# Pool multiplies the scan's states with C two at a time, with a ring of eight states

## The chip, the core and the metric

The kernel runs on one NeuronCore of a Trainium2 chip. The core has five engines with queues of their own: PE (TensorE, matrix multiply), DVE (VectorE), ACT (ScalarE), Pool (GpSimd) and SP (SyncE, which here issues all transfers). They meet by semaphores. The metric is device time in microseconds (us). The kernel before takes 12802.62 us (median of 3 runs, 12800.36 to 12805.07).

## The reference

The input is x of 8 images x 96 channels x 64 x 64 in float32. Layer 0 is a group norm, then a vision state-space block: layer norm, a projection to 192 channels and a gate, a depthwise 3x3 convolution, a selective scan along four directions, an output norm, gate and projection, and a small channel-attention convolution branch. Layer 1 is a linear attention and a feed-forward whose operands are rounded to an 8-bit float. The change lies in the selective scan and in where one weight is kept. The scan:

```python
def selective_scan(xs, dts, A, Bs, Cs, Ds, dt_bias):
    delta = jax.nn.softplus(dts + dt_bias[None, :, :, None])
    ...
    def step(h, inp):
        u_t, d_t, b_t, c_t = inp
        dA = jnp.exp(d_t[..., None] * A)
        h = dA * h + (d_t * u_t)[..., None] * b_t[:, :, None, :]
        y = jnp.einsum('bkdn,bkn->bkd', h, c_t)
        return (h, y)
    _, ys = jax.lax.scan(step, h0, (u_l, d_l, B_l, C_l))
    y = jnp.moveaxis(ys, 0, -1)
    return y + Ds[None, :, :, None] * xs
```

There are K = 4 directions (along rows, along columns, and both backwards), 192 channels, 16 states per channel and 64 x 64 = 4096 positions per image.

## The kernel before, in words

The eight images follow each other. For each, `prep_a` (norms, input projection) and `prep_b` (convolution, and the projection with w_xp that gives B, C and the low-rank dts) run, then `scan`, then `post` (all the rest). Each is a block at whose end the engines meet. w_xp (128 x 640 float32, the weights of the second projection) is built once in the setup on DVE (L434) and stays in SBUF.

`scan` makes six passes T over the 4096 positions, in four chunks of 1024: 128 channels by rows (T = 0) and by columns (T = 1), then the remaining 64 channels of both directions together (T = 2), and the same three backwards (3 to 5). T = 1 and 4 are called column-wise below. In a chunk g each of the 16 states n goes through these steps; a tile is 128 channels x 1024 positions.

- ACT: exp of delta times A[n] (`decay`, L1110), for the states in POOLED = (2, 5, 7, 10, 13, 15) into a PSUM bank instead. Exp n waits for scan n - 2. Behind exp n stands the copy of the last column of state n - 1 (`carry`, L1087), which Pool waits for, so that the multiply with C cannot overwrite it. Behind exp 3 and carry 2 stand a table load, the softplus of the next chunk and a table load back (L1093); behind exp 5 the copy of the previous chunk's y (L1080).
- B[n] times du: for ten states PE spreads the row of B over the partitions (L994) and DVE multiplies it by du (L1158). For the six in POOLED the row comes from memory by a broadcasting transfer into `b_sb` and Pool multiplies it (L1191, into `dbu`, two buffers).
- DVE: `tensor_tensor_scan` over the 1024 positions (L1171), into `state`, a ring of RING = 7 tiles. It waits until PE has added up the state that was in the slot.
- Pool: state times C[n] in place (L1202), with the row of C from memory in `c_sb` (a ring of CRING = 4). SP loads the row of n once the multiply of n - 4 is done (L942, in passes 2 and 5 two transfers of 64 partitions, L946).
- PE: adds the products of the 16 states in PSUM with an identity matmul (L1017), in an order given by SUMS_AT, six steps behind the scans and later.

du of the next chunk (delta times u, L1141) is made by DVE in front of scan 8 (DU_AT), and delta is copied by ACT after exp 9 (L1101). Both have two buffers. All orders are written out in the code, by the place of each call in the loops over n. Lines of the kernel before are used below; names such as "scan 10", "exp 4" and "carry 3" mean the instruction of that state, C(2,3) Pool's multiply of states 2 and 3, B10 Pool's B product for state 10.

Of the kernel before, what the change touches and what calls it, by code (L numbers as in the profile page):

```python
# [55 lines left out]
RING = 7  # L56
CRING = 4
# [3 lines left out]
B_AHEAD = 4  # L61
# [3 lines left out]
DU_AT = 8  # L65
# [42 lines left out]
def build(nc, x, weights, phase_weights, setup_weights, out, gate_dram, gn_dram):  # L108
    bc_dram = nc.dram_tensor("bc", (NDIR, 2, NS, L), F32, kind="Internal").ap()
# [28 lines left out]
    w_xp = put("w_xp", [128, 5, 128], F32)  # L138
# [52 lines left out]

    conv_diag = at("conv_diag", [128, PE_TAPS, 128], F32, C0 + 512 + 20480)
# [26 lines left out]
    delta, du, decay, state, c_sb, b_sb, dbu = (scan_buf(n, r) for n, r in (("delta", 2), ("du", 2), ("decay", 2), ("state", RING), ("c_sb", CRING),  # L219
# [44 lines left out]
    with ExitStack() as ctx:  # L264
# [9 lines left out]
        dbu_pooled scanned carried weighted summed y_summed y_taken c_in_0 c_in_1 c_in_2 c_in_3 b_in_0  # L274
# [91 lines left out]
        with nc.Block() as block:  # L366
            @block.sync
            def _(sp):
# [6 lines left out]
                sp.wait_ge(S["w_loaded"], 80 + 16 * GROUPS)  # L375

# [9 lines left out]
            def _(dve):  # L386
# [40 lines left out]
                for g in range(2):  # L427
                    for order in range(2):
                        places = ((w3, order, order, 0, 128), (w3, 2 + order, 2, DR * order, DR * order + DR))
                        for from_, i, src, lo_p, hi_p in places + (((w3_up, 4, 2, DR, 128),) if order == 0 else ()):  # L430
                            for to, st, first, count in ((NS * g, 2 * g, 3 * NS * order, NS),
                                                         (C_ROW + NS * g, 2 * g + 1, 3 * NS * order, NS),
                                                         (DT0 + RANK * g, 2 * g + order, 6 * NS, RANK)):
                                nc.vector.tensor_copy(w_xp[lo_p:hi_p, i, to:to + count],  # L434
                                                      from_[lo_p:hi_p, st, src, first:first + count])
# [76 lines left out]
        def prep_a(img):  # L512
            bank = dict(zip(("turn0", "turn1", "mean", "za", "var", "halo", "xi", "mix"), sum(ps, [])))
            with nc.Block() as block:  # L514
                @block.sync
                def _(sp):
# [4 lines left out]

                    sp.wait_ge(S["gn_ready"], NCH)
# [70 lines left out]
                def _(pe):  # L593
# [300 lines left out]
        def scan():  # L894
# [27 lines left out]
            def slot(g, n):  # L922

                return (g * NS + n) % RING

            def c_landed(T, c, n):

                before = sum(32 if t % 3 == 2 else 16 for t in range(T)) * (NSC * NS // CRING)
                return (c * (NS // CRING) + (n // CRING + 1)) * (32 if T % 3 == 2 else 16) + before

# [5 lines left out]
            with nc.Block() as block:  # L936
                @block.sync
                def _(sp):
# [11 lines left out]
                    def steps(T, c, previous, following):  # L950
# [4 lines left out]
                        for n in range(NS):  # L955
# [3 lines left out]
                            sp.wait_ge(S["weighted"], g * NS + n - CRING + 1 + CREDIT)  # L959
                            spread_row(T, at, 1, n, c_sb[:, n % CRING, :], f"c_in_{n % CRING}")  # L960
# [25 lines left out]
                def _(pe):  # L986
# [24 lines left out]
                    def add_up(g, n):  # L1011
# [3 lines left out]
                        pe.wait_ge(S["weighted"], g * NS + n + 1 + CREDIT)  # L1015
# [48 lines left out]
                def _(act):  # L1064
# [731 lines left out]
```

## Time and profile before

| What | us or share |
|---|---|
| profiled execution, its own time | 12802.17 |
| its span in the trace | 12800.4 |
| PE busy | 10530.1 (82%) |
| DVE busy | 11326.4 (88%) |
| ACT busy | 6529.3 (51%) |
| Pool busy | 10358.3 (81%) |
| Pool, state times C (L1202), 3072 recorded | 7180.6, mean 2375 ns |
| Pool, B times du (L1191), 1152 | 2731.8, mean 2371 ns |
| DVE, B times du (L1158), 1920 | 2320.3, mean 1208 ns |
| DVE, the scans with a carry and a decay tile (L1171), 1440 | 3378.3, mean 2346 ns |
| TensorE's granted clock, mean | 0.896 |

The busy shares are means over an image's stages, the scan and the rest. The mean of an instruction is from its start to its end as the profiler draws it; consecutive instructions of one engine can overlap there, so what one costs in a row is read from the distance of starts. PE's rows show two speeds of the same matmul, since its clock is granted at either of two levels.

### The profile page before, as it was taken

The numbers are of one execution on the slowest core, as the hardware profiler recorded it, in microseconds if no ns is written. First come the engines' busy times: TensorE is split into PE (matmuls) and PEld (weight loads), VectorE is DVE, ScalarE is ACT, GpSimd is POOL, SyncE is SP. The second block draws the span as 40 slices with busy tenths as digits, with TensorE's granted clock in tenths as the row PEclk, the third lists the DMA queues.
The fourth block names the chain that finished last, engine by engine and source line by source line (L and its number), as shares of the span: only waits on it lengthen the run. The fifth ranks groups of instructions, "written<-read, shape, count | busy, mean of one in ns | idle before, by whom it ended". The sixth has DMA issues, their size and how long they took to land. (4 is left out here: it accounts for less than half of the span.)

```text
span 12800.4 us, 92077 instructions
## 1 busy us (share of the span) xinstructions
PE 10530.1 (82%) x24646; PEld 4148.3 (32%) x24646; DVE 11326.4 (88%) x8071; ACT 6529.3 (51%) x9780; POOL 10358.3 (81%) x4597
## 2 busy tenths in 40 slices
PE   7888888788887888878888788887888888888888
PEld 2333333333333332333323333233332333333333
DVE  7999779997899978999789997899978999689996
ACT  4445455454544555455555455554555445554455
POOL 5999559994599946999469994699946999469993
PEclk9888989989899898988988889899998888989888
DMA  5787547775478744777447774577745777357773
GB/s 147 225 227 227 124 136 226 228 226 120 144 224 229 225 114 150 223 229 226 109 151 227 228 226 107 157 226 228 225 102 163 226 229 225 95 165 224 227 227 95
DMA packets 734712, 2403.47 MB, mean 188 GB/s; under 512 B 173200, under 2 KB 175248, under 8 KB 722768
## 3 DMA queue, kind: packets, MB, share of 16 engines
q1 hardware_dynamic: 734192, 2397.58, 64.5%
q8 instruction: 199, 3.26, 0.1%
q14 instruction: 321, 2.63, 0.1%
HBM read 2300.18 MB, written 67.11 MB: 185 GB/s over the span
## 5 line engine op out<-in xcount | busy, mean ns | idle before, releaser
L1202 POOL TENSOR_TENSOR state<-state,c_sb 128x1024 f32<-128x1024 f32 x3072 | 7180.6, 2375 | 71.5 <-ACT carry L1087 52.0
L1017 PE MATMUL ps<-state,wt 128*128 128x512 f32 x12288 | 6354.9, 660 | 160.9 <-ACT ya L1080 97.4
L1017 PEld LDWEIGHTS ps<-state,wt 128*128 128x128 f32 x12288 | 2564.7, 212 | 3074.0 <-issue 2483.9
L1171 DVE TENSOR_TENSOR_SCAN state<-decay,carry,ps 128x1024 f32<-128x1024 f32 x1440 | 3378.3, 2346 | 117.2 <-DVE ps L1158 72.9
L1087 ACT COPY carry<-state 128x1 f32<-128x1 f32 x3072 | 584.3, 190 | 4925.5 <-DVE state L1171 4919.1
L1191 POOL TENSOR_TENSOR dbu<-b_sb,du 128x1024 f32<-128x1024 f32 x1152 | 2731.8, 2371 | 174.3 <-DVE du L1176 174.3
L994 PE MATMUL ps<-parts,sel 114*128 114x512 bf16 (+1 forms) x3840 | 1325.0, 431 | 1658.6 <-DVE state L1171 1642.0
L1158 DVE TENSOR_TENSOR ps<-ps,du 128x1024 f32<-128x1024 f32 x1920 | 2320.3, 1208 | 26.2 <-PE ps L994 23.2
L1110 ACT ACTIVATE decay<-delta,a_neg 128x1024 f32<-128x1024 f32 x1920 | 2198.4, 1145 | 3.4 <-issue 0.3
L1171 DVE TENSOR_TENSOR_SCAN state<-ps,carry,dbu 128x1024 f32<-128x1024 f32 x864 | 2013.9, 2331 | 69.4 <-POOL dbu L1191 56.0
L994 PEld LDWEIGHTS ps<-parts,sel 114*128 114x128 bf16 (+1 forms) x3840 | 281.4, 102 | 3169.8 <-DVE state L1171 2713.5
L1110 ACT ACTIVATE ps<-delta,a_neg 128x1024 f32<-128x1024 f32 x1152 | 1283.5, 1114 | 0.0
L1171 DVE TENSOR_TENSOR_SCAN state<-decay,ps 128x1024 f32<-128x1024 f32 x480 | 1097.2, 2286 | 50.4 <-DVE ps L1158 24.3
L1518 POOL CAST h<-h16b 128x1536 fp8e5<-128x1536 f16 x64 | 116.0, 1812 | 895.9 <-DVE h16b L1643 895.9
L1171 DVE TENSOR_TENSOR_SCAN state<-ps,dbu 128x1024 f32<-128x1024 f32 x288 | 654.5, 2273 | 43.8 <-POOL dbu L1191 38.5
L302 ACT ACT_TABLE_LOAD x409 | 524.7, 1283 | 71.2 <-DMA x_tok<-x 26.9
L1504 POOL TENSOR_TENSOR sqa<-sqa,sqr 64x512 f32<-64x512 f32 x64 | 101.9, 1593 | 412.0 <-ACT sqr L1412 412.0
L1006 PE MATMUL ps<-parts,dt_w 114*128 114x512 bf16 (+1 forms) x1536 | 377.2, 389 | 43.4 <-PEq L659 29.9
L502 ACT ACTIVATE rs<-ps,wt 96x512 f32<-96x512 f32 (+1 forms) x320 | 218.4, 683 | 318.7 <-PE ps L487 172.3
L492 DVE TENSOR_TENSOR cen<-x,ps 96x512 f32<-96x512 f32 x192 | 130.6, 680 | 249.4 <-PE ps L487 248.7
L487 PE MATMUL ps<-sq,wt 96*96 96x512 f32 x512 | 281.7, 633 | 23.3 <-ACT sq L497 22.2
L704 POOL TENSOR_SCALAR conv_acc<-pad_r,wt 128x512 f32<-128x512 f32 x8 | 12.5, 1566 | 355.2 <-POOLq L514 355.2
(209 smaller groups left out, 8812.8 us busy)
## 6 DMA issues: line engine op xcount, KB each, us to landing
c_sb<-bc SPq DMA_DIRECT2D x2048, 512.0 KB, 4.4
c_sb<-bc SPq DMA_DIRECT2D x2048, 256.0 KB, 5.7
b_sb<-bc SPq DMA_DIRECT2D x768, 512.0 KB, 4.7
b_sb<-bc SPq DMA_DIRECT2D x768, 256.0 KB, 5.6
x_nat<-x SPq DMA_DIRECT2D x17, 1536.0 KB, 14.7
gates<-gate_a SPq DMA_DIRECT2D x8, 2048.0 KB, 6.8
x_tok<-x SPq DMA_DIRECT2D x288, 48.0 KB, 1.9
gn<-gn_t SPq DMA_DIRECT2D x8, 1536.0 KB, 7.1
```

What stands on the lines that cost most here:

```text
L302: act.add_instruction(mybir.InstLoadActFuncSet(name=nc.get_next_instruction_name(), act_func_set_id=which, ins=[], outs=[]))
L487: pe.matmul(bank[0:C, :], col("ones_c", C), src[0:C, sl(j)], start=True, stop=True).then_inc(done, 1)
L502: act.activation(root[:, sl(j)], bank[0:p, :], ACT.Ln, bias=col("eps", p)).then_inc(logged, 1)
L994: mm = pe.matmul(bank[:, q * CH:(q + 1) * CH], sel[own, n, first:first + 128], part_cols(at, 2 * (T // 3), q, own), start=True, stop=True)
L1006: mm = pe.matmul(pc[:, q * CH:(q + 1) * CH], dt_w[own, p, w, :], part_cols(at, k, q, own), start=(i == 0 and p == 0), stop=(i == len(ways) ...
L1017: mm = pe.matmul(py[:, q * CH:(q + 1) * CH], col("ident"), state[:, slot(g, n), q * CH:(q + 1) * CH], start=(n == 0), stop=False)
L1087: act.copy(carry[:, n:n + 1], state[:, slot(g, n), last:last + 1]).then_inc(S["carried"], 1)
L1110: act.activation(pb[n % 2][:, :] if n in POOLED else decay[:, n % 2, :], delta[:, g % 2, :], ACT.Exp, scale=a_neg[:, T, n:n + 1]).then_inc ...
L1158: dve.tensor_tensor(pb[n % 2][:, :], pb[n % 2][:, :], du[:, g % 2, :], ALU.mult)\
L1171: dve.tensor_tensor_scan(state[:, slot(g, n), way], rate, what, 0.0 if fresh else carry[:, n:n + 1], ALU.mult, ALU.add)\
L1191: pool.tensor_tensor(dbu[:, i % BRING, :], b_sb[:, i % BRING, :], du[:, g % 2, :], ALU.mult)\
L1202: pool.tensor_tensor(state[:, slot(g, n), :], state[:, slot(g, n), :], c_sb[:, n % CRING, :], ALU.mult).then_inc(S["weighted"], 1)
```

## The change

Pool takes two states in one instruction of 128 x 2048, once the carries of both have been copied. The ring of states has eight tiles, so a pair is always adjacent; C rows come in a ring of three pairs, and the semaphores `weighted` and `c_in_*` count pairs. Room for this comes from delta and du, of which there is one buffer each: du of the next chunk is made in front of scan 15, when Pool's B15 is done, and delta is copied after exp 15. The first B product of a chunk (state 2) moves to the end of the previous one, ahead of C(14,15). B rows are asked for five steps ahead rather than four. The larger scan buffers lie over w_xp, so it is stored to memory once in the setup and loaded again by SP in each `prep_a`, and the first input projection waits for that load with the others. With one buffer, L1158 and L1110 read `du[:, :]` and `delta[:, :]`; such lines are left out here.

```diff
-RING = 7
-CRING = 4
+RING = 8
+PAIR = 2
+CRING = 6
-B_AHEAD = 4
+B_AHEAD = 5
-DU_AT = 8
...
+                sp.wait_ge(S["setup_dve"], 7)
+                sp.dma_start(xp_dram, w_xp[:, :, :].rearrange("p i c -> p (i c)")).then_inc(S["w_loaded"], 16)
+                sp.wait_ge(S["w_loaded"], 96 + 16 * GROUPS)
...
+                    sp.dma_start(w_xp[:, :, :].rearrange("p i c -> p (i c)"), xp_dram).then_inc(S["w_in_loaded"], 16)
...
-                            pe.wait_ge(S["w_in_loaded"], 64)
+                            pe.wait_ge(S["w_in_loaded"], 80)
...
-                            sp.wait_ge(S["weighted"], g * NS + n - CRING + 1 + CREDIT)
-                            spread_row(T, at, 1, n, c_sb[:, n % CRING, :], f"c_in_{n % CRING}")
+                            sp.wait_ge(S["weighted"], pair_of(g, n) - CRING // PAIR + 1 + CREDIT)
+                            spread_row(T, at, 1, n, c_sb[:, PAIR * c_place(g, n) + n % PAIR, :], f"c_in_{c_place(g, n)}")
...
-                        pe.wait_ge(S["weighted"], g * NS + n + 1 + CREDIT)
+                        pe.wait_ge(S["weighted"], pair_of(g, n) + 1 + CREDIT)
...
-                        act.wait_ge(S["decayed"], max(g - 1, 0) * NS)
-                        act.copy(delta[:, g % 2, :], pc[:, :]).then_inc(S["delta_ready"], 1)
+                        act.wait_ge(S["decayed"], g * NS)
+                        act.copy(delta[:, :], pc[:, :]).then_inc(S["delta_ready"], 1)
...
-                                if n == DU_AT + 1:
+                                if n == NS - 1:
                                     delta_out(g + 1)
...
-                        dve.wait_ge(S["dbu_pooled"], (g - 1) * NP + CREDIT)
+                        dve.wait_ge(S["dbu_pooled"], g * NP + CREDIT)
...
-                            if n == DU_AT and after:
+                            if n == NS - 1 and after:
                                 next_du(*after, g + 1)
...
-                            if n + 2 in POOLED:
+                            if n > 0 and n + 2 in POOLED:
                                 times_b(T, c, POOLED.index(n + 2))
-                            pool.wait_ge(S["carried"], g * NS + n + 1 + CREDIT)
-                            pool.wait_ge(S[f"c_in_{n % CRING}"], c_landed(T, c, n))
-                            pool.tensor_tensor(state[:, slot(g, n), :], state[:, slot(g, n), :], c_sb[:, n % CRING, :],
-                                               ALU.mult).then_inc(S["weighted"], 1)
-
+                            if n == NS - 1 and following:
+                                times_b(*following, 0)
+                            if n % PAIR == PAIR - 1:
+                                times_c(T, c, n - PAIR + 1)
+
+                    def times_c(T, c, n):
+
+                        g = c + T * NSC
+                        pool.wait_ge(S["carried"], g * NS + n + PAIR + CREDIT)
+                        pool.wait_ge(S[f"c_in_{c_place(g, n)}"], c_landed(g, n))
+                        first = PAIR * c_place(g, n)
+                        both = state[:, slot(g, n):slot(g, n) + PAIR, :]
+                        pool.tensor_tensor(both, both, c_sb[:, first:first + PAIR, :], ALU.mult)\
+                            .then_inc(S["weighted"], 1)
```

Pool's order over one chunk of the kernel before, from the B product of state 2 (`dbu`) on:

```order
L1191 TENSOR_TENSOR dbu<-b_sb,du 128x1024
L1202 TENSOR_TENSOR state<-state,c_sb 128x1024 x3
L1191 TENSOR_TENSOR dbu<-b_sb,du 128x1024
L1202 TENSOR_TENSOR state<-state,c_sb 128x1024 x2
L1191 TENSOR_TENSOR dbu<-b_sb,du 128x1024
L1202 TENSOR_TENSOR state<-state,c_sb 128x1024 x3
L1191 TENSOR_TENSOR dbu<-b_sb,du 128x1024
L1202 TENSOR_TENSOR state<-state,c_sb 128x1024 x3
L1191 TENSOR_TENSOR dbu<-b_sb,du 128x1024
L1202 TENSOR_TENSOR state<-state,c_sb 128x1024 x2
L1191 TENSOR_TENSOR dbu<-b_sb,du 128x1024
L1202 TENSOR_TENSOR state<-state,c_sb 128x1024 x3
```

And of the changed kernel, from B5, behind C(0,1), to the pair after the next chunk's B2 (its x2 are C(14,15) and the next C(0,1)):

```order
L1207 TENSOR_TENSOR dbu<-b_sb,du 128x1024
L1228 TENSOR_TENSOR state<-state,c_sb 128x2048
L1207 TENSOR_TENSOR dbu<-b_sb,du 128x1024
L1228 TENSOR_TENSOR state<-state,c_sb 128x2048 x2
L1207 TENSOR_TENSOR dbu<-b_sb,du 128x1024
L1228 TENSOR_TENSOR state<-state,c_sb 128x2048
L1207 TENSOR_TENSOR dbu<-b_sb,du 128x1024
L1228 TENSOR_TENSOR state<-state,c_sb 128x2048
L1207 TENSOR_TENSOR dbu<-b_sb,du 128x1024
L1228 TENSOR_TENSOR state<-state,c_sb 128x2048
L1207 TENSOR_TENSOR dbu<-b_sb,du 128x1024
L1228 TENSOR_TENSOR state<-state,c_sb 128x2048 x2
```

Sixteen multiplies have become eight, B2 has moved in front of C(14,15), and nothing stands between C(14,15) and C(0,1), nor between C(4,5) and C(6,7).

DVE around the du of the next chunk, before: from scan 6 over scan 7, multiply 8, du (`ps2` holds softplus's output) and scan 8 to multiply 9 and its scan.

```order
L1171 SCALAR_TENSOR_TENSOR state_103<-decay_102,carry_63,ps0 128x1024
L1171 SCALAR_TENSOR_TENSOR state_103<-ps1,carry_63,dbu_106 128x1024
L1158 TENSOR_TENSOR ps0<-ps0,du_101 128x1024
L1141 TENSOR_TENSOR du_101<-ps2,ua_81 128x1024
L1171 SCALAR_TENSOR_TENSOR state_103<-decay_102,carry_63,ps0 128x1024
L1158 TENSOR_TENSOR ps1<-ps1,du_101 128x1024
L1171 SCALAR_TENSOR_TENSOR state_103<-decay_102,carry_63,ps1 128x1024
```

The changed kernel, from scan 12 to scan 0 of the next chunk, which begins a pass and so takes no carry:

```order
L1187 SCALAR_TENSOR_TENSOR state_103<-decay_102,carry_63,ps0 128x1024
L1187 SCALAR_TENSOR_TENSOR state_103<-ps1,carry_63,dbu_106 128x1024
L1174 TENSOR_TENSOR ps0<-ps0,du_101 128x1024
L1187 SCALAR_TENSOR_TENSOR state_103<-decay_102,carry_63,ps0 128x1024
L1157 TENSOR_TENSOR du_101<-ps2,ua_81 128x1024
L1187 SCALAR_TENSOR_TENSOR state_103<-ps1,carry_63,dbu_106 128x1024
L1174 TENSOR_TENSOR ps0<-ps0,du_101 128x1024
L1187 SCALAR_TENSOR_TENSOR state_103<-decay_102,ps0 128x1024
```

The du now stands between scan 14 and scan 15. ACT around softplus, in the changed kernel, from exp 3 to carry 3:

```order
L1126 ACTIVATE decay_102<-delta_100,a_neg_54 128x1024
L1103 COPY carry_63<-state_103 128x1
L304 ACT_TABLE_LOAD
L1109 ACTIVATE ps2<-ps2,wt_49 128x1024
L304 ACT_TABLE_LOAD
L1126 ACTIVATE decay_102<-delta_100,a_neg_54 128x1024
L1103 COPY carry_63<-state_103 128x1
```

This piece is as before but for its line numbers: carry 3 (the last row) stands behind exp 4.

## Rows read from the trace of the kernel before

**Rows 1.** Windows, image 1's scan: us, each engine's busy us, PEclk, DMA share, GB/s

```profile
186.00:1410.00 1224.00, 1000.67 (x2270) 390.05 (x2270) 1183.44 (x646) 609.38 (x887) 1210.63 (x524) 0.88 0.77 227
```

**Rows 2.** The timeline (start, us, instruction, idle before): first du, last copy

```profile
187.22 1.22 DVE L1176 TENSOR_TENSOR du<-ps,ua 128x1024 f32<-128x1024 f32 x1 [3.47 <-ACT ps L1093]
...
1425.50 1.01 ACT L1077 COPY y<-ps 64x1024 f32<-64x1024 f32 x1
...
11338.48 1.23 DVE L1176 TENSOR_TENSOR du<-ps,ua 128x1024 f32<-128x1024 f32 x1 [3.42 <-ACT ps L1093]
...
12576.83 1.01 ACT L1077 COPY y<-ps 64x1024 f32<-64x1024 f32 x1
```

**Rows 3.** The timeline of Pool, one chunk of pass 2

```profile
698.23 2.33 POOL L1191 TENSOR_TENSOR dbu<-b_sb,du 128x1024 f32<-128x1024 f32 x1
...
723.63 2.33 POOL L1191 TENSOR_TENSOR dbu<-b_sb,du 128x1024 f32<-128x1024 f32 x1
...
749.03 2.33 POOL L1191 TENSOR_TENSOR dbu<-b_sb,du 128x1024 f32<-128x1024 f32 x1
```

**Rows 4.** The timeline of DVE, the same chunk

```profile
700.60 2.34 DVE L1171 TENSOR_TENSOR_SCAN state<-ps,carry,dbu 128x1024 f32<-128x1024 f32 x1
...
709.87 2.33 DVE L1171 TENSOR_TENSOR_SCAN state<-ps,carry,dbu 128x1024 f32<-128x1024 f32 x1
...
717.37 2.35 DVE L1171 TENSOR_TENSOR_SCAN state<-decay,carry,ps 128x1024 f32<-128x1024 f32 x1 [0.55 <-DVE ps L1158]
...
725.99 2.35 DVE L1171 TENSOR_TENSOR_SCAN state<-ps,carry,dbu 128x1024 f32<-128x1024 f32 x1 [0.53 <-POOL dbu L1191]
...
729.50 1.22 DVE L1141 TENSOR_TENSOR du<-ps,ur 128x1024 f32<-128x1024 f32 x1
730.64 2.34 DVE L1171 TENSOR_TENSOR_SCAN state<-decay,carry,ps 128x1024 f32<-128x1024 f32 x1
...
736.40 2.33 DVE L1171 TENSOR_TENSOR_SCAN state<-ps,carry,dbu 128x1024 f32<-128x1024 f32 x1
...
751.40 2.34 DVE L1171 TENSOR_TENSOR_SCAN state<-ps,carry,dbu 128x1024 f32<-128x1024 f32 x1
```

**Rows 5.** The timeline of ACT, DVE, Pool around scan 4 of a chunk

```profile
358.48 1.15 ACT L1110 ACTIVATE decay<-delta,a_neg 128x1024 f32<-128x1024 f32 x1
359.54 0.17 ACT L1087 COPY carry<-state 128x1 f32<-128x1 f32 x1
...
359.72 2.35 DVE L1171 TENSOR_TENSOR_SCAN state<-decay,carry,ps 128x1024 f32<-128x1024 f32 x1 [0.55 <-DVE ps L1158]
...
359.79 2.34 POOL L1202 TENSOR_TENSOR state<-state,c_sb 128x1024 f32<-128x1024 f32 x1 [0.22 <-ACT carry L1087]
```

**Rows 6.** The timeline of DVE, a column-wise du

```profile
526.12 1.95 DVE L1141 TENSOR_TENSOR du<-ps,ua 128x1024 f32<-128x1024 f32 x1
```

**Rows 7.** The timeline of Pool: 128, 512 and 1024 wide

```profile
52.99 2.27 POOL L530 TENSOR_TENSOR conv_diag<-wt,conv_w 128x128 f32<-128x128 f32 x5
...
105.87 1.27 POOL L715 TENSOR_TENSOR conv_acc<-conv_acc,conv_tap 128x512 f32<-128x512 f32 x1
...
188.53 2.35 POOL L1191 TENSOR_TENSOR dbu<-b_sb,du 128x1024 f32<-128x1024 f32 x1 [21.69 <-DVE du L1176]
```

**Rows 8.** The timeline of DVE, scan 2 of the first chunk

```profile
196.45 2.27 DVE L1171 TENSOR_TENSOR_SCAN state<-ps,dbu 128x1024 f32<-128x1024 f32 x1
```

**Rows 9.** The timeline of DVE, a multiply that waited for PE

```profile
339.43 1.23 DVE L1158 TENSOR_TENSOR ps<-ps,du 128x1024 f32<-128x1024 f32 x1 [1.50 <-PE ps L994]
```

**Rows 10.** The timeline of PE, the last state's sum of image 1

```profile
1420.74 1.98 PE L1017 MATMUL ps<-state,wt 128*128 128x512 f32 x4 [0.32 <-POOL state L1202]
```

**Rows 11.** The page's DMA issues: KB each, median us to landing

```profile
c_sb<-bc SPq DMA_DIRECT2D x2048, 256.0 KB, 5.7
```

**Rows 12.** The timeline of SP and PE, image 2's w_in loads and first projection

```profile
1646.38 1.81 SPq L519 DMA_DIRECT2D w_in_sb<-phase_weights  x4
...
1659.85 1.06 PE L611 MATMUL ps<-cen,w_in_sb 96*128 96x512 f32 x2
```

More of the change, by code:

```diff
@@ L190, in build @@
     gn_work = at("gn_work", [C, 352], F32, C0 + 512 + 23552)
+    w_xp = at("w_xp", [128, 5, 128], F32, C0 + 512 + 25088)
     conv_diag = at("conv_diag", [128, PE_TAPS, 128], F32, C0 + 512 + 20480)
@@ L217, in scan_buf @@
         return at(name, [128, SC] if ring is None else [128, ring, SC], F32, first)
-    delta, du, decay, state, c_sb, b_sb, dbu = (scan_buf(n, r) for n, r in (("delta", 2), ("du", 2), ("decay", 2), ("state", RING), ("c_sb", CRING),
+    delta, du = map(scan_buf, ("delta", "du"))
+    decay, state, c_sb, b_sb, dbu = (scan_buf(n, r) for n, r in (("decay", 2), ("state", RING), ("c_sb", CRING),
                                                                  ("b_sb", BRING), ("dbu", BRING)))
@@ L433, in _ @@
                                                          (DT0 + RANK * g, 2 * g + order, 6 * NS, RANK)):
-                                nc.vector.tensor_copy(w_xp[lo_p:hi_p, i, to:to + count],
-                                                      from_[lo_p:hi_p, st, src, first:first + count])
+                                last = nc.vector.tensor_copy(w_xp[lo_p:hi_p, i, to:to + count],
+                                                             from_[lo_p:hi_p, st, src, first:first + count])
+                last.then_inc(S["setup_dve"], 1)
             @block.tensor
@@ L924, in slot, with pair_of, c_place, c_landed @@
                 return (g * NS + n) % RING
-            def c_landed(T, c, n):
-                before = sum(32 if t % 3 == 2 else 16 for t in range(T)) * (NSC * NS // CRING)
-                return (c * (NS // CRING) + (n // CRING + 1)) * (32 if T % 3 == 2 else 16) + before
+            def pair_of(g, n):
+                return (g * NS + n) // PAIR
+            def c_place(g, n):
+                return pair_of(g, n) % (CRING // PAIR)
+            def c_landed(g, n):
+                each = NSC * NS // PAIR
+                return sum((32 if p // each % 3 < 2 else 64) for p in range(pair_of(g, n) + 1)
+                           if p % (CRING // PAIR) == c_place(g, n))
             def b_landed(T, c, i):
@@ L1175, in _ @@
                     dve.wait_ge(S["delta_made"], 1)
[L1176 removed]
+                    dve.tensor_tensor(du[:, :], pc[:, :], u_of(0, 0), ALU.mult).then_inc(S["du_ready"], 1)
                     each_chunk(steps)
@@ L1190, in times_b @@
                         pool.wait_ge(S["scanned"], g * NS + last + 1 + CREDIT)
-                        pool.tensor_tensor(dbu[:, i % BRING, :], b_sb[:, i % BRING, :], du[:, g % 2, :], ALU.mult)\
+                        pool.tensor_tensor(dbu[:, i % BRING, :], b_sb[:, i % BRING, :], du[:, :], ALU.mult)\
                             .then_inc(S["dbu_pooled"], 1)
```

12 lines of the change are left out of this document (6 added, 6 removed).

## The prediction

> **What bounds the kernel now.** I read the busy table first (DVE 88%, Pool 81%, both with gaps outside the scan), then the windows, then the instructions in order of time. The window over one image's scan [rows 1] has Pool busy 1210.6 of 1224 us and DVE 1183.4: in the scan Pool never rests. In the row-wise chunks shown, Pool starts the B product of state 15 at 698.23 and again at 749.03 [rows 3], a cycle of 50.80 us in which it does 16 C multiplies and 6 B products, so it starts one each 2.309 us although each is drawn 2.33 to 2.35 long: consecutive ones overlap by some 0.04. DVE is close behind: its scans wait now and then for a B product (scan 7 started at 725.99 after 0.53 idle [rows 4], 2.36 after Pool began that product). So one engine limits and the other has about 1 us of room per chunk. Whatever the change gives Pool is worth something only until DVE, or a wait between the two, comes last.
>
> From the first du of an image to its last copy of y the scan takes 1238.3 us in the first image (187.22 to 1425.50) and 1238.4 in the last (11338.48 to 12576.83) [rows 2]; over the eight the mean is 1236.3.
>
> **The pair multiply, its price.** No 128x2048 instruction is in the trace. From below and above: alone, a 1024-wide one takes 2.35 and a 512-wide one 1.27 [rows 7], 2.11 ns per element, so 1024 more elements add 2.16 to the spacing of 2.309: 4.47. From the five 128-wide ones in 2.27 (0.45 each [rows 7]) the slope is (2.309 - 0.45) / 896 = 2.07 ns, which gives 4.43. I take P = 4.455 between starts, 4.49 until it is done. The ends of the range: 4.62 if a pair saves nothing, and 4.17 if all 0.45 us of the 128-wide one were fixed cost and one of them went. Pool's own work falls from 50.80 to 8 x 4.455 + 6 x 2.309 = 49.5 us a chunk. The Trainium skill, GPSIMD Engine Reference, section 3.1, states 4497 ns for a tensor_tensor of 2048 fp32 elements on this engine. No run here shows it yet; with 4.46 in place of 4.455 the sum below would grow by 3 us.
>
> **What a pair waits for.** It starts when the carry of its second state has been copied by ACT. For states 2 and 3 this is the costly case. ACT's order there is: exp of 3, carry 2, table load, softplus, table load, exp of 4, and only then carry 3. The trace has exp 4 at 358.48, carry 3 at 359.54, scan 4 on DVE at 359.72, and Pool starting on that carry at 359.79 [rows 5]. Now Pool takes states 0, 1, 2 one by one while this goes on, so nothing is lost; after the change state 2 waits too, and the pair (2,3) starts 0.07 after scan 4.
>
> **One chunk after the change,** from scan 2 to scan 2 of the next, in DVE's spacings [rows 4]. Scan 2 to scan 4: 709.87 to 717.37, 7.50, with DVE's stall for exp 4 in it (unchanged). Then Pool's order is C(2,3), B7, C(4,5), C(6,7), B10: scan 10 can start at 0.07 + P + 2.31 + 2P + 2.37 = 18.11 after scan 4. DVE alone would need 736.40 - 717.37 = 19.03, less 1.14 for du (which leaves this place: 729.50 to 730.64) and 0.53 of idle: 17.36. So scan 10 waits about 0.75 us for its B product: the stall of the chunk. Scan 10 to scan 15 takes 15.00 (736.40 to 751.40), scan 15 to scan 2 takes 9.27 (700.60 to 709.87), and du, now ahead of scan 15, 1.14. Sum 7.50 + 18.11 + 15.00 + 9.27 + 1.14 = 51.02. With a column-wise du, 1.95 long, 1.87 between starts [rows 6], it is 51.75; the waits for PE that such chunks have now lie between scans 4 and 10 and go under the 0.75.
>
> The others on that clock (scan 2 at 0): C(0,1) 0.39 (copy of carry 1), B5 4.84, C(2,3) 7.57 after 0.42 idle, B7 12.03, C(4,5) 14.3, C(6,7) 18.8, B10 23.24, C(8,9) 25.6, B13 30.0, C(10,11) 32.3, B15 36.8, C(12,13) 39.1, next B2 43.5, C(14,15) 45.9 to 50.3, then idle 1.1 until carry 1. Every other product is in time: B13 is done 2.5 before scan 13, B15 done at 39.1 before du at 40.6.
>
> **Single delta and du.** du can be made only when B15 is done, which it is; scan 15 goes on behind it. ACT then copies delta (no longer than the 1.15 of an exp of that size [rows 5]) and makes exp 0: done some 1.22 + 2 x 1.15 + 0.2 = 3.7 after du starts, needed behind scan 15 and multiply 0, at 1.14 + (9.27 - 2.26 - 3.50) = 4.65, where 2.26 is one scan and 3.50 a multiply with its scan. Next B2 starts at 43.5, du is done at 41.9. Cost nothing beyond the moved 1.14; without the cover of scan 15 both would cost 2.3 each chunk. **Ring of eight:** scan n waits for the sum of n - 8, which PE has two steps earlier. Nothing gained but the odd wait of scan 7 for a slow first sum in column-wise chunks.
>
> **C rows three pairs deep.** Row 11 is queued on SP behind the b row of state 15, which waits for B10 to end at 25.6. In passes 2 and 5 a row is two transfers of 256 KB that land 5.7 us after issue [rows 11]: 31.3 at the soonest, and C(10,11) is due at 32.3. SP's issuing of three transfers ahead eats that; I expect it up to 1 us late, which Pool takes from the 1.5 that B15 has to du and the 1.1 idle. Elsewhere rows have over 1.5 us to spare.
>
> **w_xp.** The reload of 320 KB is fifth behind four w_in loads issued at 1646.38; the first projection that waits for all starts at 1659.85 [rows 12]. At 5.7 us for a similar transfer [rows 11] it is hidden. The store in the setup is once, SP waits for it: 5 us.
>
> **The image.** First du to scan 2: 9.23 (187.22 to 196.45 [rows 2, 8]). 23 cycles: 15 x 51.02 + 8 x 51.75 = 1179.3. In the first chunk of a pass scans start from zero and are 0.06 shorter (2.27 against 2.33 [rows 8, 4]); on the stretches where DVE leads that is 8 of them, -0.5 a time, -3.5 in all. The end: from scan 2 of the last chunk, C(14,15) ends at 48.0 (no next B2 there), PE adds both states in 2 x 1.98, less 0.1 of overlap, and add_y and y's first copy take what they take now, 1420.74 + 1.98 to 1425.50 = 2.8 [rows 2, 10]: 54.8. Total 9.23 + 1179.3 - 3.5 + 54.8 = 1239.8 against 1236.3: +3.5, times 8 = +28. To that comes PE in its slow spells: at 339.43 DVE sat 1.50 us for a spread matmul [rows 9] while Pool's backlog covered part; with DVE leading I put 1 us more an image, +8, and +5 for the setup. +41 on the profiled run's 12802.2 us (span 12800.4; the median of the runs shown is 12802.62, the same): **12843 us**.
>
> **Rivals.** *Pool's pair is cheaper, DVE alone sets the pace (faster).* If P is near 4.17, scan 10 waits for nothing: 7.50 + 17.36 + 24.27 + 1.14 = 50.27, column-wise 51.0 plus some 0.3 of PE waits. Against the forecast -0.75 x 15 - 0.45 x 8 = -15 an image, -119: 12724. Each 0.1 us of P moves the cycle by 0.3 and the kernel by 0.3 x 184 = 55 us; below P = 4.33 the result is measurably faster. For it: Pool's instructions overlap at their ends by an amount no wider row shows. Against: both slopes above.
> *A pair costs two singles (slower).* P = 4.62: cycle +0.5, +91: 12934. For it: a two-row access may restart. Against: the fixed part that the widths show.
> *The third slot comes late (slower).* In passes 2 and 5 row 11 lands over 2.5 us after it could, B15 then delays du and scan 15: about 1 us in each of 64 chunks, +64: 12907. It decides once landing plus queueing exceeds some 8 us from B10's end.
> *A wash.* The waits that I put on the path overlap with stalls Pool or PE cause now, and the gain of the ring cancels the pair's wait: 12,790 to 12,820.
>
> **Numbers.** Less than 0.2% (26 us) cannot be told from no change here. Forecast 0.45 (two thirds of it above 12828), cheaper pair 0.20, no saving 0.12, late row 0.10, a wash 0.13. That gives faster 0.20, same 0.28, slower 0.52, and a range of 12765 to 12905.
>
> **What would show it.** Pool: starts of consecutive pairs 4.455 apart; an idle of about 0.4 before C(2,3) and 1.1 before C(0,1), both released by ACT's carry. DVE: an idle of 0.75 at scan 10, released by dbu, and cycles of 51.0 and 51.7. Wrong if Pool's pairs are under 4.35 or over 4.55, if scan 10 does not wait, or if Pool waits for c_sb.

## The result, and the profile after

The changed kernel takes 12904.2 us (median of 4 runs, 12903.4 to 12906.8) against 12803.0 for the kernel before (4 runs, 12800.4 to 12805.1): ratio 1.0079, 95% interval 1.0062 to 1.0097. It is slower by 101 us. The forecast was 12843, +41, in a range of 12765 to 12905: the sign and most of the mechanism were right, but several sizes were too small, and the time lies only 0.8 us inside the end of the range.

From the page after: the busy line of the five engines, the costliest groups that the change touches (busy us, mean ns, idle before it and its main releaser), and two rows of the DMA issues (KB each, median us to landing).

```profile
PE 10357.4 (80%) x24646; PEld 4045.0 (31%) x24646; DVE 11317.5 (88%) x8071; ACT 6563.8 (51%) x9780; POOL 10155.1 (79%) x3061
...
L1228 POOL TENSOR_TENSOR state<-state,c_sb 128x2048 f32<-128x2048 f32 x1536 | 6941.6, 4525 | 354.1 <-ACT carry L1103 296.9
...
L1207 POOL TENSOR_TENSOR dbu<-b_sb,du 128x1024 f32<-128x1024 f32 x1152 | 2716.1, 2358 | 175.9 <-DVE du L1192 131.6
...
L1174 DVE TENSOR_TENSOR ps<-ps,du 128x1024 f32<-128x1024 f32 x1920 | 2320.6, 1209 | 72.8 <-PE ps L1010 70.5
...
c_sb<-bc SPq DMA_DIRECT2D x2048, 256.0 KB, 6.7
```

Pool's C multiplies fell from 7180.6 to 6941.6 us busy, but Pool now stands idle before them for 354 us (71.5 before), 297 of them for ACT's copy of a carry and 54 for rows of C (52 and 18.5 before). A 256 KB row of C lands 6.7 us after its issue, where it was 5.7 [rows 11].

The window over image 1's scan, same columns as [rows 1]:

```profile
186.00:1410.00 1224.00, 967.59 (x2253) 371.19 (x2251) 1169.94 (x643) 611.14 (x883) 1169.32 (x329) 0.92 0.76 225
```

Pool is busy 1169.3 of 1224 us and no longer 1210.6, DVE 1169.9 and no longer 1183.4. Neither engine is full: they wait for each other. Pool's timeline (start, us, instruction, idle before and releaser) in pass 2, the place of [rows 3]: C(10,11) of a chunk, then from C(0,1) of the next one on:

```profile
704.32 4.51 POOL L1228 TENSOR_TENSOR state<-state,c_sb 128x2048 f32<-128x2048 f32 x1 [0.55 <-DMA c_sb<-bc]
...
722.86 4.52 POOL L1228 TENSOR_TENSOR state<-state,c_sb 128x2048 f32<-128x2048 f32 x1 [0.45 <-ACT carry L1103]
727.35 2.35 POOL L1207 TENSOR_TENSOR dbu<-b_sb,du 128x1024 f32<-128x1024 f32 x1
729.99 4.51 POOL L1228 TENSOR_TENSOR state<-state,c_sb 128x2048 f32<-128x2048 f32 x1 [0.29 <-ACT carry L1103]
734.46 2.35 POOL L1207 TENSOR_TENSOR dbu<-b_sb,du 128x1024 f32<-128x1024 f32 x1
736.76 8.99 POOL L1228 TENSOR_TENSOR state<-state,c_sb 128x2048 f32<-128x2048 f32 x2
745.72 2.34 POOL L1207 TENSOR_TENSOR dbu<-b_sb,du 128x1024 f32<-128x1024 f32 x1
```

C(10,11) waits 0.55 us for a row, C(0,1) 0.45 and C(2,3) 0.29 us for a carry; C(4,5) and C(6,7) take 8.96 from 736.76 to B10's start, so a pair costs 4.48. DVE in the same chunk, from du to du, the place of [rows 4]:

```profile
712.04 1.20 DVE L1157 TENSOR_TENSOR du<-ps,ur 128x1024 f32<-128x1024 f32 x1
...
729.92 2.35 DVE L1187 TENSOR_TENSOR_SCAN state<-decay,carry,ps 128x1024 f32<-128x1024 f32 x1 [0.55 <-DVE ps L1174]
...
748.09 2.35 DVE L1187 TENSOR_TENSOR_SCAN state<-ps,carry,dbu 128x1024 f32<-128x1024 f32 x1 [0.83 <-POOL dbu L1207]
...
763.12 1.20 DVE L1157 TENSOR_TENSOR du<-ps,ur 128x1024 f32<-128x1024 f32 x1
```

The cycle is 51.08 us (50.80 before). C(2,3) starts 0.07 after scan 4, and scan 10 starts 18.17 after scan 4 with 0.83 of idle for B10: the chain that the prediction worked out. The same engine in the last chunk of pass 1, a column-wise one, and in the first of pass 2, where another wait shows: multiply 8 for PE's spread of its B row (the prediction knew such a wait, of multiply 14, from [rows 9]). Then PE ahead of the first of the two:

```profile
587.76 1.23 DVE L1174 TENSOR_TENSOR ps<-ps,du 128x1024 f32<-128x1024 f32 x1 [1.30 <-PE ps L1010]
...
639.03 1.23 DVE L1174 TENSOR_TENSOR ps<-ps,du 128x1024 f32<-128x1024 f32 x1 [1.43 <-PE ps L1010]
```

```profile
580.56 6.72 PE L1033 MATMUL ps<-state,wt 128*128 128x512 f32 x8 [1.43 <-ACT ya L1096]
587.12 0.60 PE L1010 MATMUL ps<-parts,sel 114*128 114x512 bf16 x2
```

Image 1 from end to end: first du, second du and last du on DVE, last copy of y on ACT, beside [rows 2].

```profile
195.05 1.22 DVE L1192 TENSOR_TENSOR du<-ps,ua 128x1024 f32<-128x1024 f32 x1 [4.35 <-ACT ps L1109]
...
248.69 1.20 DVE L1157 TENSOR_TENSOR du<-ps,ua 128x1024 f32<-128x1024 f32 x1
...
1378.39 1.20 DVE L1157 TENSOR_TENSOR du<-ps,ur 128x1024 f32<-128x1024 f32 x1
...
1444.37 1.01 ACT L1093 COPY y<-ps 64x1024 f32<-64x1024 f32 x1
```

That is 53.6 to the second du, 1129.7 for 22 cycles and 66.0 to the end. Over the eight images the means are 53.51, 1129.21 and 66.21, together 1248.9 where before had 1236.3: +12.6 an image, +101 in all. The rest of the span moved by under 4 us.

### The profile page after: what moved, and what is told of

It is laid out like the page before. It is cut to its first block and busy times, and to the rows that moved or that the text cites. A ratio compares the mean times of both kernels' runs of the same rounds, so it can differ in the third digit from the quotient of the medians.

```text
span 12905.0 us, 89007 instructions
## 1 busy us (share of the span) xinstructions
PE 10357.4 (80%) x24646; PEld 4045.0 (31%) x24646; DVE 11317.5 (88%) x8071; ACT 6563.8 (51%) x9780; POOL 10155.1 (79%) x3061
## 5 line engine op out<-in xcount | busy, mean ns | idle before, releaser
L1228 POOL TENSOR_TENSOR state<-state,c_sb 128x2048 f32<-128x2048 f32 x1536 | 6941.6, 4525 | 354.1 <-ACT carry L1103 296.9
L1033 PE MATMUL ps<-state,wt 128*128 128x512 f32 x12288 | 6212.3, 646 | 191.9 <-ACT ya L1096 94.0
L1033 PEld LDWEIGHTS ps<-state,wt 128*128 128x128 f32 x12288 | 2489.9, 207 | 3049.7 <-issue 2391.2
L1010 PE MATMUL ps<-parts,sel 114*128 114x512 bf16 (+1 forms) x3840 | 1236.0, 406 | 1905.4 <-DVE state L1187 1903.2
L1174 DVE TENSOR_TENSOR ps<-ps,du 128x1024 f32<-128x1024 f32 x1920 | 2320.6, 1209 | 72.8 <-PE ps L1010 70.5
L1187 DVE TENSOR_TENSOR_SCAN state<-ps,carry,dbu 128x1024 f32<-128x1024 f32 x864 | 2013.9, 2331 | 76.2 <-POOL dbu L1207 75.4
L1010 PEld LDWEIGHTS ps<-parts,sel 114*128 114x128 bf16 (+1 forms) x3840 | 253.6, 98 | 3402.7 <-DVE state L1187 3159.6
L1187 DVE TENSOR_TENSOR_SCAN state<-ps,dbu 128x1024 f32<-128x1024 f32 x288 | 654.2, 2272 | 68.7 <-POOL dbu L1207 67.9
L1117 ACT COPY delta<-ps 128x1024 f32<-128x1024 f32 x192 | 194.3, 1012 | 217.8 <-DVE du L1157 217.8
L493 PE MATMUL ps<-sq,wt 96*96 96x512 f32 x512 | 281.8, 633 | 23.2 <-ACT sq L503 22.1
```

The lines of the kernel that those rows point to most:

```text
L493: pe.matmul(bank[0:C, :], col("ones_c", C), src[0:C, sl(j)], start=True, stop=True).then_inc(done, 1)
L1010: mm = pe.matmul(bank[:, q * CH:(q + 1) * CH], sel[own, n, first:first + 128], part_cols(at, 2 * (T // 3), q, own), start=True, stop=True)
L1033: mm = pe.matmul(py[:, q * CH:(q + 1) * CH], col("ident"), state[:, slot(g, n), q * CH:(q + 1) * CH], start=(n == 0), stop=False)
L1174: dve.tensor_tensor(pb[n % 2][:, :], pb[n % 2][:, :], du[:, :], ALU.mult)\
L1187: dve.tensor_tensor_scan(state[:, slot(g, n), way], rate, what, 0.0 if fresh else carry[:, n:n + 1], ALU.mult, ALU.add)\
L1228: pool.tensor_tensor(both, both, c_sb[:, first:first + PAIR, :], ALU.mult)\
```

## The experiments

Twelve kernels, each timed beside the kernel before on the same chip (its medians there 12794.8 to 12796.8). Edits are on the changed kernel unless the title says otherwise. The changed kernel was not timed again beside them, and the kernel before was 6 to 8 us faster there than in the result's 12803.0; so up to 8 us of each difference to 12904.2 may come from the chip and the time and not from the edit. "In the scans" means the eight stretches from first du to last copy of y, summed in the trace. What lies outside them is the same work in all these kernels but for the store and loads of w_xp, and yet takes 2885 to 2919 us, so some 20 us of a difference between two traces can lie there. "Idle for dbu" is the idle time of DVE in front of scans and du that Pool's B products released, "idle for PE" that in front of its multiplies, both summed over the whole trace; before has 94.5 and 23.2 us, after 144.6 and 70.5.

**e1_single: the pair as two 128x1024 multiplies, each behind its own carry.**

```diff
-                        pool.wait_ge(S["carried"], g * NS + n + PAIR + CREDIT)
...
-                        pool.tensor_tensor(both, both, c_sb[:, first:first + PAIR, :], ALU.mult)\
...
+                        for i in range(PAIR):
+                            pool.wait_ge(S["carried"], g * NS + n + i + 1 + CREDIT)
...
+                            one = state[:, slot(g, n + i), :]
+                            pool.tensor_tensor(one, one, c_sb[:, PAIR * c_place(g, n) + i, :], ALU.mult)\
```

> The changed kernel with one thing undone: Pool multiplies the two states of a pair by two 128x1024 instructions, each waiting for its own carry; place in Pool's order, ring of eight, C ring, du, delta and reload stay as in the changed kernel. Theory A (the loss is the wait of a pair for its second state, on the path carry 3 - C(2,3) - B7 - C(4,5) - C(6,7) - B10 - scan 10): Pool works 22 x 2.31 = 50.8 us a chunk and is the bound again, scan 10 no longer waits 0.85, cycles fall from 51.08 to about 50.8, time near 12850 (12820 to 12870). Rival B (the moved du, the single delta and du, or the C ring cost the time, the pairs gain some): Pool's extra 1.3 us a chunk comes on top, cycles above 51.3 and time 12950 or more.

12841.96 us, ratio 1.0036 [1.0022, 1.0051]. Theory A by its time: in this order of instructions the pair costs 62 us more than two singles (58 in the scans). Pool's idle for carries went from 297 us to 4, so the wait for the second carry costs more than the 0.14 us that a pair saves. But A's "scan 10 no longer waits" did not come true: scan 10 sat 142 us for B10 with pairs and still sits 106 with singles, and Pool waits 105 us for rows of C. The place of B10 is the larger part of that stall, and the next run moves it.

**e2_b10: B10 one place earlier, in front of C(6,7).**

```diff
+                            if n == 7:
+                                times_b(T, c, POOLED.index(10))
-                            if n > 0 and n + 2 in POOLED:
+                            if n > 0 and n + 2 in POOLED and n + 2 != 10:
```

> The changed kernel with B10, Pool's B product of state 10, one place earlier: in front of C(6,7) and not behind it. Theory A (scan 10 waits because B10 stands behind four pairs): the idle at scan 10 goes, cycles by rows fall from 51.08 to 50.25 (what DVE alone needs), Pool's idle before C(0,1) nearly vanishes, column-wise chunks and pass 5 gain less since multiply 8 waits for PE there; about 15 us an image, time 12784 (12760 to 12820). Rival B (the loss sits elsewhere, in du, delta, C rows): the idle moves to another scan and the time stays within 20 us of 12904.

12749.77 us, ratio 0.9966 [0.9953, 0.9979]. DVE's two rows for scans that take a B product from Pool, with and without a carry:

```profile
L1187 DVE TENSOR_TENSOR_SCAN state<-ps,carry,dbu 128x1024 f32<-128x1024 f32 x864 | 2011.0, 2328 | 0.0
...
L1187 DVE TENSOR_TENSOR_SCAN state<-ps,dbu 128x1024 f32<-128x1024 f32 x288 | 653.1, 2268 | 2.9 <-POOL dbu L1207 2.8
```

After, the same two rows have 75.4 and 67.9 us of that idle. It is gone at the scans (14 us of it now stand before du), and the time fell by 154, to 10 us below A's range. 151 of that lie in the scans, of which 28 in the first chunks, where scan 10 had sat 4.5 us in each image, and 123 in the cycles. Scan 10's wait was worth all of its size. The changed kernel with this one call moved is faster than the kernel before.

**e3_softplus: softplus and its table loads at state 8 rather than 3.**

```diff
+SOFT_AT = 8
...
-                                if n == PRE_AT + 1:
+                                if n == SOFT_AT:
                                     softplus(following[0], g + 1)
```

> The changed kernel with ACT's table load, softplus and table load behind exp 8 and carry 7 instead of behind exp 3 and carry 2; PE's matmuls for it stay where they are. Theory A: carry 3 comes 1.4 us sooner, C(2,3) starts straight behind B5, B10 0.4 us sooner, idle at scan 10 down from 0.85 to about 0.5, the 0.55 at scan 4 moves to scan 9; cycles by rows 50.7, about 6 us an image, time 12855 (12830 to 12880). Rival (carry 3 is not on the path, Pool's order alone is): no change, 12890 to 12915.

12845.79 us, ratio 1.0037 [1.0024, 1.0050]: -58. Theory A: DVE's wait for the late exp moved to scan 9 as it said (58.2 us in all where it was 96.6 at scan 4), and scan 10's wait fell from 142 us to 116.

**e4_sp_order: B rows asked for behind both C rows of a pair, C rows ahead of the late transfers of the first chunk.**

```diff
-B_AHEAD = 5
+B_AT, NEXT_B_AT = {1: 5, 3: 7, 7: 10, 9: 13, 11: 15}, 13
...
-                            if n + B_AHEAD in POOLED:
-                                spread_b(T, at, g, POOLED.index(n + B_AHEAD))
...
+                            if n in B_AT:
+                                spread_b(T, at, g, POOLED.index(B_AT[n]))
```

> The changed kernel with another order of SP's loads: the B row of a pooled state is asked for behind both C rows of a pair and never between them (B10 from five to three steps ahead), and in the first chunk of an image the C row goes ahead of the late transfers. Nothing else moves. Theory C (of the 101 us, some 34 are the first chunk of each image, where Pool waits 3.3 us for C rows 6 and 7 queued behind a B row that waits for B5 and behind the late transfers, and some 10 are late C rows in passes 2 and 5): first chunk 53.6 down to about 50, time 12868 (12845 to 12885). Rival (the rows are late because of the transfers' own time, not their place in the queue): within 10 us of 12904.

12872.16 us, ratio 1.0060 [1.0047, 1.0073]: -32, theory C by its time. The first chunk shortened less than it said, from 53.5 to 51.4 us in the mean and not to 50: 17 us of the 32. The cycles and the end give 5 more, and the rest lies outside the scans, where the edit changes nothing. The first chunk on Pool in the changed kernel:

```profile
218.57 4.53 POOL L1228 TENSOR_TENSOR state<-state,c_sb 128x2048 f32<-128x2048 f32 x1
226.43 4.51 POOL L1228 TENSOR_TENSOR state<-state,c_sb 128x2048 f32<-128x2048 f32 x1 [3.34 <-DMA c_sb<-bc]
230.90 2.33 POOL L1207 TENSOR_TENSOR dbu<-b_sb,du 128x1024 f32<-128x1024 f32 x1
```

C(6,7) sits 3.34 us for its rows, B10 stands behind it, and DVE's scan 10 follows at 233.27 after 4.55 of idle.

**e6_reload_only: the kernel before with only the store and the reloads of w_xp.**

```diff
+                sp.dma_start(xp_dram, w_xp[:, :, :].rearrange("p i c -> p (i c)")).then_inc(S["w_loaded"], 16)
...
+                    sp.dma_start(w_xp[:, :, :].rearrange("p i c -> p (i c)"), xp_dram).then_inc(S["w_in_loaded"], 16)
```

> The kernel before, with only the store of w_xp in the setup and its reload in each image added. Theory A (the reload is hidden in every image, the store costs once): 2 to 10 us over the kernel before, and PE's first input projection of an image starts as long after the w_in loads as before (13.5 us in image 2). Rival (the reload delays each image's first projection, or the loads behind it on SP): 30 us or more over the kernel before, with PE waiting for w_xp ahead of that projection.

12797.49 against 12796.59 us, ratio 1.0002 [0.9993, 1.0011], which is -9 to +14 us: the rival's 30 is out, and A's 2 to 10 cannot be told from nothing. The reload is hidden: from an image's last copy of y to the next first du the mean is 357.2 us and was 357.1.

**e7_soft_first: e2_b10 with softplus and its table loads in front of carry 2 instead of behind it.**

```diff
+                            if following and n == PRE_AT + 1:
+                                softplus(following[0], g + 1)
                             if n > 0:
                                 carry_on(T, g, n - 1)
...
-                                if n == PRE_AT + 1:
-                                    softplus(following[0], g + 1)
```

> The changed kernel with B10 in front of C(6,7) (as in the run before this one, 12750 us) and, in addition, ACT's softplus with its two table loads one place earlier: behind exp 3 and in front of carry 2. Theory A: exp 4 then starts 1.3 + 3.7 after scan 1 instead of 3.7 after scan 2's end, so the 0.55 at scan 4 (in every chunk but the last of an image) goes; C(2,3) still waits for carry 3, which comes sooner. DVE would need 49.6 a chunk by rows, Pool 49.7, so cycles fall from 50.15 to about 49.75: some 8 us an image, 12685 (12660 to 12715). Rival (PE's dt matmuls come too late for the earlier softplus, or carry 2 held back delays a scan or Pool): 12740 or more.

12652.25 us, ratio 0.9888 [0.9874, 0.9901]: the fastest of all. Its gain over e2_b10 is 97.5 us and the time lies below A's range. The idle of DVE that late exps caused is gone (95.6 in e2_b10, none here), some of it came back before du (14 to 25 us, for B15), and in the scans 80 us were gained. The other 18 lie outside them, where TensorE's granted clock between two scans was 0.921 against 0.914: they are not the edit's work as far as the traces tell. A pair waits for its second carry anyway, so here the first may come late. Pool's timeline, one chunk from B15 to B15:

```profile
700.10 2.38 POOL L1207 TENSOR_TENSOR dbu<-b_sb,du 128x1024 f32<-128x1024 f32 x1
...
749.76 2.39 POOL L1207 TENSOR_TENSOR dbu<-b_sb,du 128x1024 f32<-128x1024 f32 x1
```

49.66 us: 8 x 4.475 + 6 x 2.31. In this chunk Pool does not rest.

**e8_before_b10: the kernel before with e2's edit.**

> The kernel before with the same move, B10 one multiply earlier (before C(7)). Theory A: here Pool does 22 x 2.31 us a chunk without a pause and the order of its work gives it nothing; cycles stay at 50.8, time within 15 us of the kernel before. Rival (the early B10 is worth its time by itself, pairs or not): 40 us or more faster than before.

12790.91 against 12794.82 us, ratio 0.9999 [0.9990, 1.0008]: A. What a place in Pool's order is worth depends on the kernel: 154 us after the change, nothing before it.

**e9_double_du: delta and du doubled again and made at state 8, paid for with a ring of only two C pairs.**

```diff
-CRING = 6
+CRING = 4
...
-                            if n == NS - 1 and after:
+                            if n == DU_AT and after:
```

> The changed kernel with du and delta in two buffers each and made at state 8 as in the kernel before, paid for with a C ring of two pairs in place of three; pairs, ring of eight and Pool's order as in the changed kernel. Theory A: du (1.14) moves back into the stretch from scan 4 to scan 10, in which DVE waits 0.85 for B10, and goes under that wait: cycles 51.08 down to about 50.3 if the C rows are in time, 12790; a row is then asked for 6.8 us (a B product and a pair) before it is due and lands 5.1 to 6.7 after issue, so part of it may be lost to Pool waiting for C: 12780 to 12900. Rival (single du costs nothing, third C slot is what matters): 12930 or more.

13127.19 us, ratio 1.0261 [1.0247, 1.0275]: the rival, and my A missed. Pool's row for the pairs:

```profile
L1228 POOL TENSOR_TENSOR state<-state,c_sb 128x2048 f32<-128x2048 f32 x1536 | 6946.6, 4527 | 594.7 <-DMA c_sb<-bc 450.2 <-ACT carry L1103 91.1 <-DVE state L1187 48.4
```

The third C slot is what makes the pair bearable: Pool's idle for C rows was 54 us with three and is 450 with two, and cycles of passes 2 and 5 are 55.2 us, with three 51.0 and 51.1. The room is better spent on the slot than on the second du. What the single du costs by itself no run separates, since both were changed here.

**e10_best: e7_soft_first with e4's order of loads and the sum of state 1 one step later** (`(0,), (1,), (2,), (3,)` in SUMS_AT becomes `(0,), (), (1, 2), (3,)`), so that PE has less in front of the spread for multiply 8.

> All edits together: B10 in front of C(6,7), softplus ahead of carry 2, B rows behind both C rows of a pair and late transfers behind the C row, and PE's sum of state 1 one step later (so that the spread matmul for state 8, for which DVE's multiply 8 waits 0.4 to 1.0 us in passes 1, 2, 4 and 5, comes ahead of it). Theory A: cycles 49.8 in all passes but the column-wise ones (50.5), first chunk 2 us shorter: 12640 (12610 to 12680). Rival (Pool, now with no idle left, takes over and the PE waits were hidden under it): the same as with the first two edits alone.

12674.65 us, ratio 0.9906 [0.9892, 0.9919]. Inside A's range, but A's way was missed: it is slower than e7 by 22 and not faster. The wait moved from multiply 8 to multiply 9 (idle for PE 57.8, in e7 61.9), and the first chunk became longer, 52.0 us where e7 has 50.0.

**e12_e7_sp: e7_soft_first with e4's order of loads alone.**

> e7_soft_first with e4_sp_order's order of loads, state 1's sum back in its place (so e10_best without the edit of the sums). Theory A (the moved sum was what hurt e10_best, the order of loads helps the first chunk as it did in e4_sp_order): 12,620 to 12,645 us, first chunk of an image 2 to 3 us shorter than in e7_soft_first, multiply 9 no longer waits. Rival (the later B rows are what hurt, since they come close to their products once nothing else is late): 12,660 us or more, with Pool waiting for b_sb in several passes.

12660.16 us, ratio 0.9892 [0.9879, 0.9906]: the rival's bound is just met, and A falls. Pool's row for the B products:

```profile
L1205 POOL TENSOR_TENSOR dbu<-b_sb,du 128x1024 f32<-128x1024 f32 x1152 | 2729.6, 2369 | 203.2 <-DVE du L1190 87.9 <-DMA b_sb<-bc 87.7 <-issue 27.6
```

In e7 that row has 174.9 of idle, all for du: the wait of an image's first B product. Here the same eight waits are 175.6 us, put down half to du and half to the row, so they cost nothing new. New are the 27.6, all before B10 in the first chunk ("issue": the profile names no releaser):

```profile
224.17 2.35 POOL L1205 TENSOR_TENSOR dbu<-b_sb,du 128x1024 f32<-128x1024 f32 x1 [4.72 <-issue]
```

The row for B10 was asked for at 209.19 and landed at 223.71. So the order of loads that shortened the first chunk of the changed kernel by 2.1 us lengthens it here by 1.9 (50.0 to 51.9): with B10 earlier, its row is due earlier too. In the scans that order costs 23 us against e7; the 8 us between the two medians are too few to be told from nothing by themselves. Nor is the moved sum what made e10 slower still: its scans are 14 us shorter in sum than those here, its stretches outside them 22 us longer, and 14 us lie between the two medians. What the moved sum is worth stays open.

**e13_single_e7: e7_soft_first with the pairs split again, as in e1_single.**

> e7_soft_first with each pair split again in two 128x1024 multiplies, each behind its own carry; ring of eight, one delta and du, the order of Pool otherwise as in e7_soft_first. Theory A (with the two waits gone the pair is what makes Pool cheaper, 8 x 0.14 us a chunk, and Pool with 22 single instructions comes back to 50.8 us a chunk or more): 12,740 to 12,850 us. Rival (the gain of e7_soft_first comes from the order alone, and singles have it too): 12,640 to 12,700 us, with cycles under 50.5.

12782.44 us, ratio 0.9989 [0.9980, 0.9998]: A. Pool from B15 to B15, and DVE's du at that place:

```profile
703.42 2.34 POOL L1208 TENSOR_TENSOR dbu<-b_sb,du 128x1024 f32<-128x1024 f32 x1
...
754.26 2.34 POOL L1208 TENSOR_TENSOR dbu<-b_sb,du 128x1024 f32<-128x1024 f32 x1
```

```profile
749.80 1.22 DVE L1158 TENSOR_TENSOR du<-ps,ur 128x1024 f32<-128x1024 f32 x1 [1.01 <-POOL dbu L1208]
```

50.84 us for 22 singles, against 49.66 with pairs: 1.18 a chunk, 0.147 a pair. In this order the pair is worth 130 us (111 of them in the scans); in e1_single's order it was worth -62.

**e14_before_soft: the kernel before with e7's place of softplus.**

> The kernel before with softplus and its table loads in front of carry 2 rather than behind it. Theory A (that kernel is bound by Pool's 22 instructions a chunk, and DVE's wait at scan 4 is under them): within 15 us of the kernel before, the idle at scan 4 gone or shorter, the idle before scans of B products longer. Rival (the softplus in front of carry 3 costs the kernel before as much as it costs the changed one): 60 us or more below the kernel before.

12977.79 us, ratio 1.0141 [1.0128, 1.0155]: +181, which neither theory had. DVE's late exp did go, but single C2 needs carry 2, now behind softplus. Pool there:

```profile
361.49 2.36 POOL L1202 TENSOR_TENSOR state<-state,c_sb 128x1024 f32<-128x1024 f32 x1 [0.80 <-ACT carry L1087]
```

That is idle in a chunk of the engine that sets the pace. Over the eight images C(2) waits so in 184 chunks, 1.09 us in the mean; Pool's idle for carries rose from 52 to 238 us, and the scans together by 187. DVE pays it as idle for dbu, 368.4 us where it was 94.5. The place that gains about 80 to 97 us with pairs costs 181 with singles.

## Why the prediction was right, and where its sizes were off

**The pair.** 4.48 between starts for the 4.455 taken, within 4.17 to 4.62; three pairs lie between scan 4 and scan 10, so by the prediction's own slope (55 us for 0.1) these 0.025 are 14 us; the slope from 512 to 1024 wide, 4.47, was the better of the two. The Trainium skill, GPSIMD Engine Reference, section 3.1, states 4497 ns for this size; the trace draws 4525 in the mean. The cheaper pair and the pair without a saving are both out (e13: 0.147 saved of 2 x 2.31).

**What it waits for.** C(2,3) 0.07 after scan 4 and idle 0.29 (0.42 expected), scan 10 idle 0.83 (0.75), row-wise cycle 51.08 (51.02). The idle before C(0,1) is 0.45 in the chunk shown, behind a pair that was 0.55 late for its row; over all chunks it is 211 us, the 1.1 a chunk expected. e1, e2 and e7 show that these waits are on the path: 62 us net of what it saves for the pair's own waits, 154 for the place of B10, 97 for that of softplus (80 in the scans). Most of scan 10's wait hangs on B10's place behind four pairs and not on the second carry: with singles 106 of its 142 us stay.

**Single delta and du.** Next exp, B2 and scan 15 were all in time, as worked out. Whether the exchange for a C slot is a good one was not weighed; e9 shows that it is.

**The third slot.** Row 11 did come late in passes 2 and 5: Pool stood for it in 30 chunks of 64, 21 us in all (0.55 in the chunk shown), and it was absorbed in C(0,1)'s idle. "Pool waits for c_sb" was named as a sign of being wrong; it does, 54 us, the rest of them nearly all in the first chunks. The rival that priced row 11 at +64 did not come about, though its time, 12907, is nearest to the one measured: the sum has to be read by its terms, since the right total can come from the wrong cause.

**The first chunk: a term left out.** I costed it by a normal chunk: 9.23 to scan 2 (measured 195.05 to 204.28, 9.23) and 40.6 - 0.5 to du, 49.3. Measured 53.51: +4.2, eight times +34. C rows are queued there behind a B row that waits for B5 and behind the transfers that fill `parts`, which I did not put on SP's clock; scan 10 sits 4.5 us in that chunk for it. This is the largest miss. e4 gives back 2.1 of the 4.2 by the order of loads (51.4 in its mean), e2 3.5 by taking B10 out from behind C(6,7) (50.0).

**The cycles: the pair and the waits for PE mis-sized.** 22 cycles, 1125.3 and an allowance of 1 for PE in the working, took 1129.2: +2.9, or +23. The pair's price explains 14 of them, as above. The rest fits the step "the waits for PE that such chunks have now lie between scans 4 and 10 and go under the 0.75". They lie there, but at 1.30 and 1.43 us they are longer than what was to cover them, and the second of these chunks is not even column-wise: idle for PE went from 23.2 to 70.5 us, 66 of it at multiply 8 (9 before) and over half of that in passes 2 and 5. In these two chunks scan 10 starts 18.67 and 18.44 us after scan 4, not 18.17. At the row of 587.76, PE's spread for multiply 8 had stood behind the sums of states 0 and 1 (6.72 us at the lower clock), and these behind ACT's copy of the previous y. That such waits hardly showed before because scan 7's wait for B7 [rows 4] stood in front of them is argued, not shown: in the five kernels whose scan 7 waits for B7 (76 us or more in all) multiply 8 waits at most 14 us for PE, in the others multiply 8, or 9 in e10, waits 54 to 71; but the five are also the ones that make du at state 8. e10 shows only that moving one sum moves the wait.

**The end.** 66.2 from the last du against 65.2: +8. Scan 15 now has a whole pair and its sums behind it: from its start to the last copy of y it takes 15.25 us in image 1 (1429.12 to 1444.37), before 11.69 (1413.81 to 1425.50).

**Setup and reload.** 5 allowed; e6 has +0.9 with an interval of -9 to +14, so it shows no cost and does not rule the 5 out.

The sum: +34, +23 and +8 over the forecast's 41, less 1 outside the images, is 105, the difference of the two spans (12905.0 - 12800.4). All the misses have one sign and add up to more than the forecast; that the range still held the time owes something to luck.

**A ledger that gives the same.** DVE does the same work in both kernels (11326.4 and 11317.5 us). So its idle in the scan plus the end tells the difference: idle in front of scans, multiplies and du 313 to 393 without the first du of an image (+80: dbu +50, PE +41, carries -10), the end +3.6 an image in image 1 (+28), busy -9: +99 of 101.

## What to carry to other kernels

Before merging two instructions into one, ask what each half waited for: the merged one starts with the later of them, and everything queued behind it on its engine moves too. Here the merge spares Pool 1.2 us a chunk, and yet the kernel lost some 60 us by it in one order of instructions and gained 130 in another. Once the merged form stands, the order around it has to be found anew: the same two edits are worth 0 and -181 us in the old kernel and +154 and +97 in the new one (the last 80 in the scans), and a fix for one wait (the order of loads, 2.1 us off each first chunk) turned into a loss (1.9) when another was mended. Check where in the span a gain lies before giving it to an edit: several differences here were partly in stages that the edit does not touch. To price it, keep a ledger of the idle of the engine whose work does not change, by releaser.

## What I had not expected of the hardware

- Rows of C land later in the changed kernel, though the traffic is the same (225 and 227 GB/s in the windows): 6.7 us for 256 KB and no longer 5.7. It is not the asking in pairs alone, since e4, with pairs and another order of loads, has 5.7 again; with two slots (e9) it was 4.8, while Pool waited far more. Time to landing tells little by itself; when a row is asked for tells more.
- The mean granted clock of TensorE rose from 0.896 to 0.92 with the change and stayed there with singles (0.921 in e1, 0.922 in e13), while the kernel before with one edit had 0.898 or 0.899. So it goes with the ring, the orders or the place of du and not with the pair. e9, with pairs and the ring of eight but du back at state 8, had 0.905. Which of them it is no run separates; nor does one tell what it is worth in the scans.
